# Flamingo gated cross-attention block: x loaded a second time in transposed form, the queries projected from it with centred weights, and the order of the steps rewritten

## The chip, the cores and the metric

One core of a Trainium2 chip. The metric is the device time of one execution in microseconds (us). The kernel before takes 1874.98 us, the median of 3 runs (1874.72 to 1876.57).

## The reference, cut to what matters

`x` is 64 x 128 x 256, the context `c` as well, all float32. There are 16 heads of 16 columns.

```python
x = x + tanh(g_xattn) * xattn(layernorm(x), c, c)     # causal, softmax, Wo, bo
x = x + tanh(g_ffn) * ffn(layernorm(x))
# layernorm(x) = (x - mean) / sqrt(var + 1e-5), over the 256 columns
# xattn: scores = (q Wq)(k Wk)^T / sqrt(16), masked above the diagonal
# ffn: h = silu(x w1 s1) * (x w2 s2); h = gelu(h h1 s); h = gelu(h h2 s); h w3 s
#      256 -> 1024 -> 1024 -> 1024 -> 256
```

## The kernel before, in words

**Blocks and stages.** The 64 batches go in 32 blocks of two (ROWS = 2, 256 tokens). A block passes two stages, attention and FFN. One pass of the loop, `body(n)`, runs attention of block n, FFN of block n-1 and the head of the attention of block n+1 (its loads, its projections, its first scores), interleaved. The passes -1 and 0 have no FFN and bring in the weights; the last two leave parts out.

**The order.** The string ORDER holds 203 steps, written out by hand as one list. Every engine walks the same list in its own loop and picks the steps it has a part in, so one list sets the order on each engine and on SP's DMA queue. Nothing else schedules: engines meet only through semaphores. `L2.3` is step L2 with index 3; a `+` means the next block. On TensorE: L1 (index 0 to 7, eight matmuls each), L2 and L3 (0 to 7, sixteen each), L4 (0 to 3, eight each) are the FFN layers, line 925; each hidden value is held in two parts, hi and lo, and multiplied twice, so a block has 352 FFN matmuls. Q, K, V project (line 860), X transposes normalised x (line 870), S.u writes the scores of eight heads to two banks (line 899), PV.t multiplies probabilities with v (line 916), To and X2 transpose (line 1011), O projects the output (line 860). The f32 matmuls of line 860 appear in the trace as two instructions each, so Q is 8 instructions and O.0 is 4.

**What surrounds them.** On ACT: a1 is tanh of L1's result (line 794), h writes ha_hi (785), a2 and a3 are Gelu to `full` and to hi (769, 771), e.t is four exps (749), x, q, k, v, to, x2 evacuate PSUM. ACT loads a function table when it goes from Gelu to Exp and back; Tanh and Exp share one, copies need none. On DVE: g and f are the two products of the gated layer (597, 604), w2 and w3 write the lo part of a pair (611), s.t masks and scales scores (570), m.t is the maximum and the exp's bias (577, 579), nh.u sums heads (588, 590), st takes mean and variance of x (530 to 536), nx normalises x (541), o.k adds the residual and takes the statistics of x1 (669 to 677), n2 normalises x1 (683), x2 writes x2T_lo (688), y scales the FFN output. On POOL: l.k writes ha_lo (476), p.t splits probabilities in two f16 parts (442, 444), nm divides heads, st and n2 are the powers -1/2 (484, 487), v writes the third part of v (465), rx adds the bias to the residual, z adds the residual of the FFN. On SP: lx, lr, lc load x, the residual and c; kw, qw write the parts of k and q to DRAM and kr, qr read them back spread over the partitions (`place_parts`); D.t transposes p_parts to pT; mv copies x1; sy stores y; W.k loads weights.

**Banks.** The steps To, O, X2, X, Q, K and V (MISC_STEPS) take turns on two PSUM banks in the order of the list; `before_step` (line 242) makes each wait until the step two places before it has been evacuated. The FFN has three banks, `before_ffn` (269) waits in the same way; PV has one bank, the scores two.

**The chain for the queries.** SP loads x_in; DVE takes the statistics (`head_stats`), POOL the power, DVE normalises x_in in place (`head_norm`), TensorE transposes it (X+), ACT copies it to xT (x+), TensorE projects it (Q+) in one step of both column halves, ACT and DVE write q's hi and lo part, SP writes and places them for S.0.

**Waits of TensorE that matter.** L2.0 waits for l.0 to l.7 one tile after another (`tile_split`); L3.0 waits for w2.0 to w2.3, one before each pair of tiles (four matmuls to a pair), so the last comes before its thirteenth matmul; L4.k waits for w3.k; L1.0 waits for x2.1 on DVE; a1.k with k over 3 waits for l.(k-4); a3.6 waits for w3.1.

In the passes -1 and 0, ACT rounds eleven weight chunks (`round_chunk`, 727) and DVE tests their low bits (635, 638), at the steps W.k; the first FFN step waits for all of them.

Of the kernel before, what the change touches and what calls it, by code (L numbers as in the profile page):

```python
# [47 lines left out]
def program(nc, x, cT_in, g_xattn, g_ffn, attn_w, bo, w_all, s1, s2, h1s, h2s, w3s, out):  # L48
# [27 lines left out]
    with ExitStack() as ctx:  # L76
# [432 lines left out]
        def _(dve):  # L509
            dve.wait_ge(pool_const, 7)  # L510
# [33 lines left out]
            def split_head(n, kind):  # L544

                parts, hi_ready, lo_ready = (q_parts, q_hi_ready, q_lo_ready) if kind == "q" else \
                    (k_parts, k_hi_ready, k_lo_ready)
                wait(dve, hi_ready, n + 1)
                dve.tensor_tensor(parts[:, 1],
                                  work[step_bank(kind.upper())][:].rearrange("p (m r t) -> p r m t", m=KE, r=ROWS),  # L550
                                  parts[:, 0].bitcast(F32), ALU.subtract).then_inc(lo_ready, 1)
# [158 lines left out]
        def _(act):  # L710
# [18 lines left out]
            def head_step(n, kind):  # L729
                use = step_bank(kind.upper())  # L730
                src = work[use][:].rearrange("p (m t) -> p m t", m=KE)
                if kind == "x":

                    wait(act, xT_ready, n + 1)
                    wait(act, q_ready, n)
                    act.activation(xT[:], src, ACT.Copy).then_inc(xT_copied, 1)
                if kind in ("q", "k"):

                    wait(act, q_ready if kind == "q" else k_ready, n + 1)
                    wait(act, q_written if kind == "q" else k_written, 16 * n)  # L740
                    act.activation((q_parts if kind == "q" else k_parts)[:, 0],
                                   work[use][:].rearrange("p (m r t) -> p r m t", m=KE, r=ROWS), ACT.Copy)\
                        .then_inc(q_hi_ready if kind == "q" else k_hi_ready, 1)
# [112 lines left out]
        def _(pe):  # L856
# [6 lines left out]
            def head_step(n, kind, k):  # L863
                bank_ = work[step_bank(kind, k)]
                before_step(pe, n, kind, k)
                if kind == "X":
                    wait(pe, xn_ready, ROWS * n + ROWS)
                    for kt in range(KE):
                        for b in range(ROWS):
                            last = pe.transpose(bank_[:, (kt * ROWS + b) * P:(kt * ROWS + b + 1) * P],  # L870
                                                x_in[:, b, kt * P:(kt + 1) * P], ident[:])
                    last.then_inc(xT_ready, 1)
                if kind in ("Q", "K"):
# [2 lines left out]
                    w, src = (wq, xT) if kind == "Q" else (wk, cT)
# [206 lines left out]
```

## Time and profile before

| | |
|---|---|
| median of 3 runs | 1874.98 us |
| profiled execution, its own time | 1874.17 us |
| its span, first to last instruction | 1872.4 us |
| mean granted TensorE clock | 0.981 |
| busy: PE, PEld, ACT, DVE, POOL | 95, 91, 65, 64, 48% |
| DMA engines, mean busy share of the steady slices | 0.4 |
| chain that ended last | PE 67%, POOL 12%, issue 9%, DVE 7% |

How to read it: times are in us unless marked ns; PE is TensorE's matmuls, PEld its weight loads, L925 is line 925 of the kernel. Matmuls overlap: a row of 0.28 us starts 0.12 us after the one before it, so distances between starts tell more than durations. The execution shown was profiled; 1.8 us of its time lie outside the span.

### The profile page before, as it was taken

The numbers are of one execution on the slowest core, as the hardware profiler recorded it, in microseconds if no ns is written. First come the engines' busy times: TensorE is split into PE (matmuls) and PEld (weight loads), VectorE is DVE, ScalarE is ACT, GpSimd is POOL, SyncE is SP. The second block draws the span as 40 slices with busy tenths as digits, with TensorE's granted clock in tenths as the row PEclk, the third lists the DMA queues.
The fourth block names the chain that finished last, engine by engine and source line by source line (L and its number), as shares of the span: only waits on it lengthen the run. The fifth ranks groups of instructions, "written<-read, shape, count | busy, mean of one in ns | idle before, by whom it ended". The sixth has DMA issues, their size and how long they took to land.

```text
span 1872.4 us, 47622 instructions
## 1 busy us (share of the span) xinstructions
PE 1781.1 (95%) x15746; PEld 1708.9 (91%) x15746; DVE 1198.4 (64%) x2706; ACT 1221.9 (65%) x2952; POOL 901.5 (48%) x1131
## 2 busy tenths in 40 slices
PE   2489999999999999999999999999999999999998
PEld 2389999999999999999999999999999999999998
DVE  3857666567666567666667766667766667766652
ACT  2566666677666677666667666667666667666664
POOL 2544544455544455544455554455454455454441
PEclk7689999999999999999999999999999999999999
DMA  6834444444445443445443444444444444444430
GB/s 227 250 86 119 124 118 131 105 119 105 124 117 134 109 117 99 129 113 139 112 120 98 123 117 131 119 116 105 119 118 123 126 110 108 116 123 118 126 55 18
DMA packets 395102, 223.04 MB, mean 119 GB/s; under 512 B 286784, under 2 KB 377152, under 8 KB 393536
## 3 DMA queue, kind: packets, MB, share of 16 engines
q1 hardware_dynamic: 390336, 222.38, 45.1%
q10 hardware_dynamic: 4736, 0.28, 0.2%
q8 instruction: 17, 0.28, 0.1%
q14 instruction: 13, 0.11, 0.0%
HBM read 105.14 MB, written 41.94 MB: 79 GB/s over the span
## 4 chain that ended last, share of the span: by engine, by line
PE 67%; POOL 12%; issue 9%; DVE 7%; ACT 3%; ACTq 1%; DMA 1%; POOLq 1%; SPq 0%; DVEq 0%
PE ffn L925 49%; PE work L860 11%; POOL ha_lo L476 8%; POOL y L493 2%; DVE negmax L577 2%; DVE probs L570 2%; PE s_bank L899 2%; PE pv L916 2%; ACT probs L749 2%; PE work L1011 1%; POOL p_parts L442 1%; DVE ha_lo L611 1%; ACTq L720 1%; PE work L870 1%; DMA pT<-p_parts 0%
## 5 line engine op out<-in xcount | busy, mean ns | idle before, releaser
L925 PE MATMUL ffn<-ha_hi,W 128*128 128x256 f32 x2048 | 500.8, 286 | 19.3 <-POOL ha_lo L476 19.3
L925 PE MATMUL ffn<-hb_hi,W 128*128 128x256 f32 x2048 | 513.7, 291 | 1.2 <-DVE hb_lo L611 1.2
L925 PE MATMUL ffn<-ha_lo,W 128*128 128x256 f32 x2048 | 488.7, 279 | 0.0
L925 PE MATMUL ffn<-hb_lo,W 128*128 128x256 f32 x2048 | 488.1, 279 | 0.0
L925 PEld LDWEIGHTS ffn<-ha_hi,W 128*128 128x128 f32 x2048 | 384.1, 188 | 28.3 <-POOL ha_lo L476 26.0
L749 ACT ACTIVATE probs<-probs,exp_bias 128x128 f32<-128x128 f32 x1024 | 320.9, 390 | 113.4 <-DVE exp_bias L579 111.9
L925 PEld LDWEIGHTS ffn<-hb_hi,W 128*128 128x128 f32 x2048 | 384.5, 188 | 4.0 <-DVE hb_lo L611 1.6
L925 PEld LDWEIGHTS ffn<-hb_lo,W 128*128 128x128 f32 x2048 | 384.8, 188 | 2.4
L925 PEld LDWEIGHTS ffn<-ha_lo,W 128*128 128x128 f32 x2048 | 384.6, 188 | 0.0
L444 POOL TENSOR_TENSOR p_parts<-probs,p_parts 128x512 f16<-128x512 f32 x256 | 313.2, 1224 | 20.5
L442 POOL CAST p_parts<-probs 128x512 f16<-128x512 f32 x256 | 159.2, 622 | 327.7 <-ACT probs L749 311.3
L769 ACT ACTIVATE full<-ffn,h2s_col 128x256 f32<-128x256 f32 x256 | 121.7, 475 | 224.2 <-PE ffn L925 223.8
L925 PE MATMUL ffn<-x2T_hi,W 128*128 128x256 f32 x1024 | 252.1, 287 | 6.2 <-issue 4.2
L925 PE MATMUL ffn<-x2T_lo,W 128*128 128x256 f32 x1024 | 245.1, 280 | 0.0
L454 POOL TENSOR_TENSOR heads<-head_sum,rden 128x128 f32<-128x128 f32 x128 | 57.2, 447 | 338.6 <-DVE head_sum L590 338.6
L925 PEld LDWEIGHTS ffn<-x2T_hi,W 128*128 128x128 f32 x1024 | 193.6, 189 | 12.6 <-DVE x2T_lo L688 5.8
L476 POOL TENSOR_TENSOR ha_lo<-full,ha_hi 128x256 fp32r<-128x256 f32 x256 | 184.2, 736 | 36.6 <-ACT ha_hi L785 33.4
L611 DVE TENSOR_TENSOR hb_lo<-full,hb_hi 128x512 fp32r<-128x512 f32 x128 | 93.9, 733 | 165.6 <-ACT hb_hi L771 165.6
L925 PEld LDWEIGHTS ffn<-x2T_lo,W 128*128 128x128 f32 x1024 | 193.8, 189 | 0.0
L611 DVE TENSOR_TENSOR ha_lo<-full,ha_hi 128x512 fp32r<-128x512 f32 x128 | 88.1, 688 | 139.4 <-ACT ha_hi L771 139.4
L577 DVE TENSOR_REDUCE negmax<-probs 128x4 f32<-128x512 f32 x256 | 173.3, 677 | 2.2
L570 DVE SCALAR_TENSOR_TENSOR probs<-s_bank,causal 128x512 f32<-128x512 f32 x256 | 166.6, 681 | 9.4 <-PE s_bank L899 7.4
(86 smaller groups left out, 3169.1 us busy)
## 6 DMA issues: line engine op xcount, KB each, us to landing
k<-k_saved SPq DMA_DIRECT2D x256, 128.0 KB, 2.9
q<-q_saved SPq DMA_DIRECT2D x256, 128.0 KB, 2.7
k_saved<-k_parts SPq DMA_DIRECT2D x32, 512.0 KB, 3.1
q_saved<-q_parts SPq DMA_DIRECT2D x32, 512.0 KB, 2.6
wnat<-in_ffn_w SPq DMA_DIRECT2D x11, 1024.0 KB, 7.0
x_in<-in_x SPq DMA_DIRECT2D x32, 256.0 KB, 2.9
cT<-in_ctx_T SPq DMA_DIRECT2D x32, 256.0 KB, 2.7
xres<-in_x SPq DMA_DIRECT2D x32, 256.0 KB, 2.7
```

Source lines behind the costliest of these rows:

```text
L442: pool.tensor_copy(p_parts[:, t % 2, 0], probs[:, t % PSLOTS]).then_inc(p_hi_ready, 1)
L444: pool.tensor_tensor(p_parts[:, t % 2, 1], probs[:, t % PSLOTS], p_parts[:, t % 2, 0], ALU.subtract)\
L454: pool.tensor_tensor(heads[:, b, at:at + PAIR * D].rearrange("p (h d) -> p h d", h=PAIR), head_sum[:, u % 2], rden[:, b, (u % 2) * PAIR:(u ...
L476: pool.tensor_tensor(ha_lo[:, k], full[:, k % 4], ha_hi[:, k], ALU.subtract)\
L493: pool.tensor_tensor(y[:, k], y[:, k], x1_prev[:, k], ALU.add).then_inc(y_ready, 1)
L570: dve.scalar_tensor_tensor(probs[:, slot], s_bank[t % SBANKS][:].rearrange("p (h t) -> p h t", h=4), SCALE, causal[:].unsqueeze(1).broadca ...
L577: dve.tensor_reduce(negmax[:, slot], probs[:, slot], AX_X, ALU.max, negate=True).then_inc(max_ready, 1)
L611: dve.tensor_tensor(lo[:, 2 * p:2 * p + 2], f, hi[:, 2 * p:2 * p + 2], ALU.subtract)\
L749: last = act.activation(probs[:, slot, h], probs[:, slot, h], ACT.Exp, bias=exp_bias[:, slot, h:h + 1])
L769: act.activation(full[:, 2 * (p % 2) + r], src, ACT.Gelu, scale=scales[:, m:m + 1])\
L860: last = pe.matmul(dst, lhsT(kt), rhs(kt), start=kt == 0, stop=kt == KE - 1)
L925: return pe.matmul(dst, w, h, **flags)
```

## The change

- The host lays out x a second time, transposed (`x_T`, per block 128 x 2 x 256). SP loads it to xT (`load_xT`, step lt+). X+, x+ and nx+ are gone: no normalisation of x ahead of the projection, no transposes, no copy.
- The mean goes into the weights: at the start TensorE takes the mean of wq over its input rows (a matrix of 1/256 times wq) and DVE subtracts it (`centre_queries`). 1/std goes into the mask: `mask` scales by rstd instead of the constant SCALE, which is folded into var_eps; st+ on POOL also waits for the masks of the block before.
- Q+ becomes Q.0+ and Q.1+, each one column half of 128 in its own bank, and so do q.0+ and q.1+ on ACT and DVE.
- The whole list ORDER is new. Both orders, as they stand, and the core of the diff:

```diff
-    W.0 l.0 W.1 s.2 s.3 kr.1 lx+ D.0 D.1 e.0 e.1 g.0 f.0 L1.0 L1.1 a1.0 a1.1 l.1 L1.2 g.1 h.0 a1.2 f.1 g.2 L1.3 L1.4
-    L1.5 f.2 h.1 g.3 L1.6 a1.3 S.2 h.2 f.3 L1.7 a1.4 h.3 l.2 l.3 PV.0 PV.1 g.4 a1.5 L2.0 f.4 l.4 h.4 L2.1 g.5 l.5
-    a1.6 h.5 f.5 g.6 a1.7 h.6 W.2 f.6 h.7 g.7 f.7 L2.2 L2.3 L2.4 l.6 l.7 m.2 L2.5 m.3 W.3 W.4 p.2 s.4 s.5 p.3 nh.0
-    D.2 m.4 st+ X+ m.5 e.2 e.3 nx+ PV.2 D.3 w2.0 PV.3 W.5 e.4 e.5 nh.1 a2.0 w2.1 S.3 a2.1 a2.2 L2.6 s.6 mv To.0 x+
-    L2.7 a2.3 a2.4 nm.0 lc+ p.4 s.7 O.0 m.6 nm.1 D.4 D.5 to.0 w2.2 K+ m.7 a2.5 L3.0 L3.1 PV.4 PV.5 L3.2 a2.6 p.5 p.6
-    p.7 Q+ sy V+ w2.3 a2.7 L3.3 L3.4 PV.6 PV.7 W.6 L3.5 e.6 To.1 D.6 o.0 L3.6 X2.0 e.7 kw+ k+ a3.0 w3.0 D.7 a3.1
-    nh.2 O.1 W.7 q+ qw+ a3.2 a3.3 W.8 L3.7 nh.3 nm.2 n2.0 kr.0+ nm.3 qr.0+ v+ lr+ W.9 a3.4 qr.1+ S.0+ L4.0 w3.1 w3.2
-    o.1 to.1 W.10 a3.5 X2.1 x2.0 L4.1 L4.2 L4.3 n2.1 rx+ S.1+ p.0+ s.0+ z.0 z.1 a3.6 m.0+ a3.7 w3.3 s.1+ m.1+ x2.1
-    y.0 y.1 p.1+
+    kr.1 W.0 e.0 L1.0 L1.1 e.1 lt+ L1.2 L1.3 a1.0 W.1 L1.4 L1.5 D.0 D.1 L1.6 p.1 s.2 s.3 L1.7 PV.0 PV.1 S.2 l.0 l.1
+    g.0 L2.0 lc+ f.0 W.2 g.1 a1.1 h.0 f.1 W.3 D.2 D.3 a1.2 g.2 f.2 g.3 l.2 h.1 a1.3 l.3 L2.1 L2.2 lx+ L2.3 f.3 h.2
+    g.4 a1.4 L2.4 f.4 h.3 g.5 a1.5 L2.5 h.4 f.5 g.6 S.3 a1.6 f.6 h.5 g.7 f.7 l.4 m.2 a1.7 h.6 h.7 e.2 m.3 e.3 PV.2
+    PV.3 l.5 nh.0 L2.6 L2.7 l.6 l.7 s.4 s.5 a2.0 a2.1 a2.2 K+ p.2 w2.0 p.3 m.4 mv nm.0 L3.0 a2.3 W.4 W.5 e.4 D.4 m.5
+    e.5 nh.1 D.5 s.6 L3.1 To.0 PV.4 w2.1 PV.5 L3.2 s.7 O.0 Q.0+ m.6 m.7 Q.1+ w2.2 w2.3 a2.4 L3.3 W.6 p.4 p.5 W.7 V+
+    PV.6 nm.1 a2.5 a2.6 a2.7 k+ e.6 PV.7 L3.4 p.6 p.7 nm.2 e.7 to.0 To.1 W.8 kw+ L3.5 o.0 q.0+ O.1 L3.6 L3.7 D.6
+    q.1+ a3.0 D.7 nh.2 W.9 st+ W.10 nh.3 w3.0 S.0+ nm.3 qw+ kr.0+ X2.0 X2.1 v+ n2.0 o.1 sy a3.1 n2.1 w3.1 to.1 w3.2
+    qr.0+ a3.2 a3.3 L4.0 L4.1 s.0+ lr+ L4.2 a3.4 qr.1+ rx+ m.0+ p.0+ w3.3 a3.5 a3.6 a3.7 x2.0 L4.3 s.1+ m.1+ x2.1
+    S.1+ y.0 y.1 z.0 z.1
```

```diff
             def load_x(n):
 
-                hold(xT_ready, n)
+                hold(stats_ready, ROWS * n)
                 sp.dma_start(x_in[:], x[bass.ds(n * ROWS, ROWS)].rearrange("b p e -> p b e")).then_inc(x_loaded, 16)
+
+            def load_xT(n):
+
+                hold(q_ready, KE * n)
+                sp.dma_start(xT[:], xT_in[bass.ds(n, 1)].rearrange("a p k t -> p (a k) t")).then_inc(xT_loaded, 16)
...
-            load_x(0)
+            load_xT(0)
             sp.dma_start(aw[:].rearrange("p w k e -> p (w k e)"), attn_w[:, :]).then_inc(attn_w_in, 16)
             load_c(0)
+            load_x(0)
...
                     if kind == "st" and here:
                         wait(pool, var_ready, blk + 1)
+                        wait(pool, masked_ready, NQ * blk)
                         pool.tensor_tensor(rstd[:], var_eps[:], minus_half[:], ALU.pow).then_inc(rstd_ready, 1)
...
-                dve.tensor_scalar(var_eps[:], moments[:, :, 1], EPS, None, ALU.add).then_inc(var_ready, 1)
-
-            def head_norm(n):
-                wait(dve, rstd_ready, n + 1)
-                for b in range(ROWS):
-                    dve.tensor_scalar(x_in[:, b], x_in[:, b], moments[:, b, 0:1], rstd[:, b:b + 1],
-                                      ALU.subtract, ALU.mult).then_inc(xn_ready, 1)
...
+                dve.tensor_scalar(var_eps[:], moments[:, :, 1], EPS, 1.0 / SCALE ** 2, ALU.add, ALU.mult)\
+                    .then_inc(var_ready, 1)
+
+            def centre_queries():
+
+                dve.wait_ge(attn_w_in, 16)
+                dve.wait_ge(wq_mean, 1)
+                dve.tensor_tensor(wq, wq, ffn[1][:, 0:E].unsqueeze(1).broadcast_to([P, KE, E]), ALU.subtract)\
+                    .then_inc(wq_centred, 1)
+
+            def split_query(n, m):
+
+                wait(dve, q_hi_ready, KE * n + m + 1)
+                dve.tensor_tensor(q_parts[:, 1, :, m],
+                                  work[step_bank("Q", m)][:, 0:TOK].rearrange("p (r t) -> p r t", r=ROWS),
+                                  q_parts[:, 0, :, m].bitcast(F32), ALU.subtract).then_inc(q_lo_ready, 1)
...
-                dve.scalar_tensor_tensor(probs[:, slot], s_bank[t % SBANKS][:].rearrange("p (h t) -> p h t", h=4), SCALE,
+                if t == 0:
+                    wait(dve, rstd_ready, n + 1)
+                dve.scalar_tensor_tensor(probs[:, slot], s_bank[t % SBANKS][:].rearrange("p (h t) -> p h t", h=4),
+                                         rstd[:, t // QROW:t // QROW + 1],
                                          causal[:].unsqueeze(1).broadcast_to([P, 4, P]), ALU.mult, ALU.add)\
...
-                if kind == "X":
-                    wait(pe, xn_ready, ROWS * n + ROWS)
-                    for kt in range(KE):
-                        for b in range(ROWS):
-                            last = pe.transpose(bank_[:, (kt * ROWS + b) * P:(kt * ROWS + b + 1) * P],
-                                                x_in[:, b, kt * P:(kt + 1) * P], ident[:])
-                    last.then_inc(xT_ready, 1)
...
+                if kind == "Q":
+                    if isinstance(n, int) and n == 0:
+                        pe.wait_ge(wq_centred, 1)
+                    wait(pe, xT_loaded, (n + 1) * 16)
+                    project(bank_[:, 0:TOK], lambda kt: wq[:, kt, k * P:(k + 1) * P], lambda kt: xT[:, kt])\
+                        .then_inc(q_ready, 1)
...
                 if first == 0:
+                    pe.wait_ge(attn_w_in, 16)
+                    project(ffn[1][:, 0:E], lambda kt: mean_of[:], lambda kt: wq[:, kt]).then_inc(wq_mean, 1)
                     body(-1, ffn_on=False, attn=False)
```

The evacuation of the queries on ACT (`queries`) is split by column half as on DVE.

## Rows read from the trace of the kernel before

**Rows 1.** The page, busy time: engine, us (share of the span), instructions.

```profile
PE 1781.1 (95%) x15746; PEld 1708.9 (91%) x15746; DVE 1198.4 (64%) x2706; ACT 1221.9 (65%) x2952; POOL 901.5 (48%) x1131
```

**Rows 2.** Busy time by stretches: stretch, length, engines, clock, DMA share, GB/s.

```profile
165.30:1783.90 1618.60, 1599.09 (x14275) 1539.44 (x14271) 1060.86 (x2437) 1093.45 (x2669) 803.78 (x1016) 1.00 0.45 117
```

**Rows 3.** Timeline of PE: start us, us, engine, line, operation.

```profile
1014.31 0.60 PE L870 MATMUL work<-ident,x_in 128*128 128x128 f32 x4
1014.75 0.57 PE L916 MATMUL pv<-vs,pT 128*128 128x49 bf16 x16
...
1740.44 0.60 PE L870 MATMUL work<-ident,x_in 128*128 128x128 f32 x4
```

**Rows 4.** Timeline of PE from the end of L1.7 into L2.0.

```profile
1057.20 0.58 PE L916 MATMUL pv<-vs,pT 128*128 128x49 bf16 x16
1057.62 0.37 PE L925 MATMUL ffn<-ha_hi,W 128*128 128x256 f32 x1
1057.83 0.28 PE L925 MATMUL ffn<-ha_lo,W 128*128 128x256 f32 x1
...
1059.28 0.28 PE L925 MATMUL ffn<-ha_lo,W 128*128 128x256 f32 x1
1060.15 0.39 PE L925 MATMUL ffn<-ha_hi,W 128*128 128x256 f32 x1 [0.59 <-POOL ha_lo L476]
```

**Rows 5.** Timeline of POOL, the last ha_lo of the same block.

```profile
1059.37 0.72 POOL L476 TENSOR_TENSOR ha_lo<-full,ha_hi 128x256 fp32r<-128x256 f32 x1 [0.37 <-ACT ha_hi L785]
```

**Rows 6.** Timeline of PE, S.1 and the first matmul of L1.

```profile
1048.05 0.66 PE L899 MATMUL s_bank<-k,q 64*128 64x128 f32 x8
1048.78 0.39 PE L925 MATMUL ffn<-x2T_hi,W 128*128 128x256 f32 x1
```

**Rows 7.** Timeline of PE: O.0 behind L2.7, a projection of 8, L3.0.

```profile
1019.94 1.02 PE L860 MATMUL work<-aw,oT 128*128 128x256 f32 x4
1020.80 1.89 PE L860 MATMUL work<-cT,aw 128*128 128x256 f32 x8
1022.34 0.47 PE L925 MATMUL ffn<-hb_hi,W 128*128 128x256 f32 x1
```

**Rows 8.** Timeline of ACT and DVE: a2.7, the table load, exps, w2.3.

```profile
1020.92 0.48 ACT L769 ACTIVATE full<-ffn,h1s_col 128x256 f32<-128x256 f32 x1
1021.28 0.48 ACT L771 ACTIVATE hb_hi<-ffn,h1s_col 128x256 fp32r<-128x256 f32 x1
1021.78 1.28 ACT L749 ACT_TABLE_LOAD   x1
1023.08 2.46 ACT L749 ACTIVATE probs<-probs,exp_bias 128x128 f32<-128x128 f32 x8
...
1021.79 0.69 DVE L611 TENSOR_TENSOR hb_lo<-full,hb_hi 128x512 fp32r<-128x512 f32 x1 [0.72 <-ACT hb_hi L771]
```

**Rows 9.** Timeline of ACT at the start.

```profile
18.14 1.28 ACT L722 ACT_TABLE_LOAD   x1 [18.14 <-issue]
```

**Rows 10.** Groups by line: busy us, mean ns | idle before, releaser.

```profile
L604 DVE SCALAR_TENSOR_TENSOR full<-ffn,half_s,full 128x256 f32<-128x256 f32 x256 | 123.9, 484 | 9.0
L597 DVE SCALAR_TENSOR_TENSOR full<-full,ffn 128x256 f32<-128x256 f32 x256 | 107.4, 419 | 37.8 <-ACT full L794 34.6
L465 POOL TENSOR_TENSOR vs<-v_rest,vs 128x512 bf16<-128x512 f32 x32 | 50.7, 1584 | 48.5 <-DVE vs L563 48.5
L487 POOL TENSOR_TENSOR rstd<-var_eps,minus_half 128x1 f32<-128x1 f32 x64 | 36.6, 572 | 98.3 <-DVE var_eps L677 98.3
```

**Rows 11.** Waits: who waited for whom, us in total, times, longest.

```profile
ACT probs L749 <- DVE exp_bias L579: 111.9, 119, 6.2
PE ffn L925 <- POOL ha_lo L476: 19.3, 33, 0.6
```

**Rows 12.** Timeline of SP and PE: the placing of q's first row, S.0.

```profile
1035.58 2.46 SPq L327 DMA_DIRECT2D q<-q_saved  x4
1043.35 0.66 PE L899 MATMUL s_bank<-k,q 64*128 64x128 f32 x8
```

More of the change, by code:

```diff
@@ L102, in program @@
         ones = sb("ones", [P, 1])
+        mean_of = sb("mean_of", [P, P])
         minus_half = sb("minus_half", [P, ROWS])
@@ L363, in body @@
                         load_x(blk)
+                    if kind == "lt" and here and not (isinstance(blk, int) and blk < 2):
+                        load_xT(blk)
                     if kind == "lr" and here:
@@ L387, in _ @@
             load_x(1)
+            load_xT(1)
             load_c(1)
@@ L418, in _ @@
             pool.memset(minus_half[:], -0.5).then_inc(pool_const, 1)
-            pool.wait_ge(pool_const, 4)
+            pool.memset(mean_of[:], 1.0 / E).then_inc(pool_const, 1)
+            pool.wait_ge(pool_const, 5)
             pool.affine_select(out=ident[:], in_=ident[:], compare_op=ALU.not_equal, fill=1.0, base=0,
@@ L509, in _ @@
         def _(dve):
-            dve.wait_ge(pool_const, 7)
+            dve.wait_ge(pool_const, 8)
             def scale_constants():
@@ L535, in head_stats, with split_keys @@
                 wait(dve, moments_ready, ROWS * n + ROWS)
-                dve.tensor_scalar(var_eps[:], moments[:, :, 1], EPS, None, ALU.add).then_inc(var_ready, 1)
-            def head_norm(n):
-                wait(dve, rstd_ready, n + 1)
-                for b in range(ROWS):
-                    dve.tensor_scalar(x_in[:, b], x_in[:, b], moments[:, b, 0:1], rstd[:, b:b + 1],
-                                      ALU.subtract, ALU.mult).then_inc(xn_ready, 1)
[L544 to L551, printed above, removed]
+                dve.tensor_scalar(var_eps[:], moments[:, :, 1], EPS, 1.0 / SCALE ** 2, ALU.add, ALU.mult)\
[10 more added lines that the diff above has]
+                                  q_parts[:, 0, :, m].bitcast(F32), ALU.subtract).then_inc(q_lo_ready, 1)
+            def split_keys(n):
+                wait(dve, k_hi_ready, n + 1)
+                dve.tensor_tensor(k_parts[:, 1],
+                                  work[step_bank("K")][:].rearrange("p (m r t) -> p r m t", m=KE, r=ROWS),
+                                  k_parts[:, 0].bitcast(F32), ALU.subtract).then_inc(k_lo_ready, 1)
             def values(n):
@@ L646, in body @@
                         head_stats(blk)
-                    if kind == "nx" and here:
-                        head_norm(blk)
-                    if kind == "nx" and isinstance(n, int) and n == -1:
+                    if kind == "st" and isinstance(n, int) and n == -1:
                         scale_constants()
@@ L691, in body @@
                             .then_inc(x2lo_ready, 1)
-                    if kind in ("q", "k") and here:
-                        split_head(blk, kind)
+                    if kind == "q" and here:
+                        split_query(blk, k)
+                    if kind == "k" and here:
+                        split_keys(blk)
                     if kind == "v" and here:
                         values(blk)
+            centre_queries()
             body(-1, ffn_on=False, attn=False)
@@ L727, in round_chunk, with queries, keys @@
                 act.activation(W[:, i * CHUNK:(i + 1) * CHUNK], wnat[:, i % STAGES], ACT.Copy).then_inc(chunk_rounded, 1)
[L729 to L743, printed above, removed]
+            def queries(n, m):
+                wait(act, q_ready, KE * n + m + 1)
+                wait(act, q_written, 16 * n)
+                act.activation(q_parts[:, 0, :, m],
+                               work[step_bank("Q", m)][:, 0:TOK].rearrange("p (r t) -> p r t", r=ROWS), ACT.Copy)\
+                    .then_inc(q_hi_ready, 1)
+            def keys(n):
+                wait(act, k_ready, n + 1)
+                wait(act, k_written, 16 * n)
+                act.activation(k_parts[:, 0],
+                               work[step_bank("K")][:].rearrange("p (m r t) -> p r m t", m=KE, r=ROWS), ACT.Copy)\
+                    .then_inc(k_hi_ready, 1)
             def exps(n, t):
@@ L836, in body @@
                             .then_inc(x2hi_ready, 1)
-                    if kind in ("x", "q", "k") and here:
-                        head_step(blk, kind)
+                    if kind == "q" and here:
+                        queries(blk, k)
+                    if kind == "k" and here:
+                        keys(blk)
                     if kind == "v" and here:
@@ L865, in head_step @@
                 before_step(pe, n, kind, k)
[L866 to L873 removed]
+                if kind == "Q":
[4 more added lines that the diff above has]
+                        .then_inc(q_ready, 1)
+                if kind == "K":
                     if isinstance(n, int) and n == 0:
                         pe.wait_ge(attn_w_in, 16)
[L876 to L877 removed]
+                    wait(pe, cT_loaded, (n + 1) * 16)
                     for m in range(KE):
[L879 to L881 removed]
+                        last = project(bank_[:, m * TOK:(m + 1) * TOK], lambda kt: wk[:, kt, m * P:(m + 1) * P],
+                                       lambda kt: cT[:, kt])
+                    last.then_inc(k_ready, 1)
                 if kind == "V":
@@ L1029, in run @@
                 body(BLOCKS, attn=False, next_head=False)
-            pe.wait_ge(pool_const, 7)
+            pe.wait_ge(pool_const, 8)
             run(False, 0)
@@ L1061 @@
         "x": x,
+        "x_T": x.reshape(b // ROWS, ROWS * s, e // P, P).transpose(0, 3, 2, 1),
         "ctx_T": ctx.reshape(b // ROWS, ROWS * s, e // P, P).transpose(0, 3, 2, 1),
```

20 lines of the change are left out of this document (8 added, 12 removed).

## The prediction

> **What bounds the kernel now.** I read the page first. TensorE is busy 95% of the span and the next engine 65% [rows 1], so the question is whether it is really full. The busy time by stretches says so for the steady part: between 165.3 and 1783.9 us it is busy 99% at a granted clock of 1.00, while DVE, ACT and POOL are at 66, 68 and 50% [rows 2]. A busy PE hides short waits, though, so I went to the order of instructions in one block and read starts, not durations. The transposes of x start at 1014.31 us in one block and at 1740.44 us 13 blocks later [rows 3]: (1740.44 - 1014.31) / 13 = 55.86 us a block. The FFN matmuls start 0.12 us apart (12 of them from 1057.83 to 1059.28) [rows 4], so 352 are some 42 us; the reader should see that this stream, the attention matmuls between its pieces and a few gaps are the whole block.
>
> Two gaps matter. In L2.0 one matmul starts at 1059.28 and the next at 1060.15, 0.75 us late; the waits put it down to POOL's ha_lo (19.3 us in 33 times) [rows 11], and the matmul behind it starts 0.1 us late too, as behind every interruption (0.21 instead of 0.12 after PV) [rows 4]: 0.86 us a block. POOL's last ha_lo began at 1059.37 and had itself waited for ACT's ha_hi [rows 5], the end of the chain L1.7, a1.7, g.7, f.7, h.7, l.7. And from S.1 to the next L1 pass 0.73 us, more than the 0.66 of its eight matmuls [rows 6], though elsewhere a group starts some 0.07 before the last one ends: 0.14 us.
>
> **The change part by part.** All against the profiled execution, 1874.17 us, 0.04% below the median of 1874.98.
>
> Removed, transposes of x: 1014.31 to 1014.75, 0.44 us of PE a block [rows 3], on the path in full. With it go the copy of xT on ACT and two normalisations on DVE; both engines have a third of their time free, so I count nothing for them.
>
> The query projection in two steps: eight half-matmuls become four and four at the same 0.216 us (O.0: 0.86 us for four), no more PE work. ACT and DVE each evacuate twice 256 columns instead of once 512, about 0.1 us of fixed cost each, covered by their idle time. But the first step of a pair frees the other's bank late: Q.1 takes O.0's bank and waits for o.0 on DVE, and starts 2 x 0.86 us after O.0 [rows 7]. o.0 needs O.0's four matmuls, 0.9 us or so with its drain, and 0.48 us of its own: nearly equal. I take 0.1 us; ends 0 and 0.5.
>
> The mask now scales by a column (rstd) and not by a constant. Nearest rows: 484 ns with a column against 419 ns with a constant, both on 256 columns [rows 10]. So 0 to 0.07 us more for each of 8 masks a block, on DVE with its slack: nothing, as long as it does not sit in the chain named below.
>
> Moved, S.2: it stood between L1.6 and L1.7 and now follows L1.7 and PV.1. The chain from L1.7's last matmul (1057.20) to POOL's last ha_lo (1059.37 + 0.72 = 1060.09) is 2.89 us; TensorE needs 0.42 for PV and 1.8 for the first seven tiles of L2.0, hence the gap [rows 4, 5]. With another 0.6 to 0.7 us of S.2 in it the gap shrinks to 0.05 to 0.15. In exchange L1.7 and PV.0 come 0.7 us earlier against f.4 and the transposed probabilities, which may be late: bounds 0 and 0.7, and I take 0.2 for what is left of both. Moved, x2.0 and X2.0: together with X2.1 ahead of L4.0. DVE then has x2.0 behind it before s.1, and X2.1 no longer lies inside L4, so L4 and S.1 run with DVE ahead of them: the 0.14 us go.
>
> Interruptions of the FFN stream per block fall from 13 to 10 (counted in the two orders), each return costs 0.09 us [rows 4], but PV in front of S gives 0.08 back: -0.2.
>
> Moved, st: POOL's rstd goes from between p.3 and p.4 to between nm.2 and nm.3, and now also waits for the masks; nm.3 waits behind it, and To.1 for nm.3. DVE runs st between nh.2 and nh.3, when V is still on TensorE, so the 0.7 us are covered; without that cover they would be on the path.
>
> The queue of SP: the load of x^T takes the place of the load of x ahead of D.0, the load of x goes behind D.3, c ahead of D.2, and the store of y between kr.0 and qr.0. Each is one issue of about 0.4 us. The placing of q is issued until 1035.58 + 2.46 = 1038.04 and S.0 starts at 1043.35 [rows 12]: 5.3 us are left for the last piece to land, and a store more in front takes 0.4 of them. Covered. 0.25 MB more a block is nothing on DMA engines busy 45% [rows 2].
>
> Two more table switches on ACT: e.4 and e.5 now stand between a2.3 and a2.4, so Gelu, Exp, Gelu. A switch costs 1.30 us: gelu ends 1021.76, load 1021.78 to 1023.06, exp starts 1023.08 [rows 8]. Between the ends of L2.3 and L2.7 TensorE has four steps of 1.89 and S.3 and PV, 8.6 us; ACT has a2.2 and a2.3 (four activations 0.36 apart), a switch, eight exps (2.46), a switch, a2.4 and a2.5: 1.4 + 1.3 + 2.5 + 1.3 + 1.4 = 7.9. It arrives 0.7 us early [rows 8]. K alone now stands between L2.7 and L3.0, so w2.3 (done 1022.48, 2.54 after L2.7's end) is wanted after K and twelve matmuls of L3.0: 8 x 0.216 + 12 x 0.118 = 3.15 us, 0.6 us to spare [rows 7, 8]. Cost nothing; if the cover of 0.7 + 0.6 us is gone, every further us is on the path. The Trainium skill (ScalarE: Activation LUTs, What ACT_TABLE_LOAD costs) puts 1380 ns of drain on top of 1283 ns of load for every switch; the load agrees with the row, the drain does not show in it. By that page two more switches last 2.76 us longer than the rows have them, and the sum would be about 1881 us.
>
> The start: Q waited for xT until 20.27 us, since ACT's first load comes at 18.14 [rows 9]; now K and Q.0 are done by then and only Q.1 is left, 1.4 us gained. Against it, the weight tests W.3 and W.10 move ahead of m.2 and of nh.3, and To.1, O.1, o.1, n2.1 then run one after another behind W.10. I take +3 us; ends -1.4 and +6.
>
> Sum a block: -0.44 (X) - 0.86 (ha_lo) - 0.14 (S.1) - 0.2 (interruptions) + 0.3 (0.2 left of the moved S.2, 0.1 for Q.1) = -1.34. Over 31 blocks with the transposes in 30: -41.5 + 0.4, with the start +3: -38. **1874 - 38 = 1836 us.**
>
> **The rivals.**
> (a) The end of the block becomes the chain. w3.0, V's evacuation (1.1), POOL's third part of v (1.6), rstd2 (0.6), n2.0 (0.4), o.1 with its statistics (1.2), rstd2 (0.6), n2.1 (0.4) and w3.1 (0.7) are now one file on DVE and POOL (POOL's pieces from [rows 10]; DVE's are estimates, 0.4 to 0.5 us for 256 columns and 0.7 for 512, after [rows 8, 10]), and a3.6 waits for w3.1, then e.0, p.0, p.1 and all of l. With w3.0 starting 1.6 us behind PV.7 that is 8.9 us; TensorE reaches the end of L3.7 after four steps, To.1 and O.1, about 8.9 us too. A slip of 0.5 us comes back whole in L2.0: 1836 + 31 x 0.5 = 1852. For it: no slack, and it is DVE and POOL work in a row. Against: none of these engines is full.
> (b) The ha_lo gap stays, because p.1 ahead of l.0 sets it and not L1.7. Then 0.66 of the 0.86 us stay: 1836 + 20 = 1856. Against: POOL waited for ACT before its last ha_lo [rows 5].
> (c) Slower: L3.0 waits for ACT. If each switch also drained for as long as it loads (2 x 1.3) and e.4 waited for its bias as the exps do now (111.9 us in 119 waits, 0.94 each [rows 11]), w2.3 slips 3.5 us against a cover of 1.3: 2.2 us a block, 1836 + 69 = 1905. The point of no gain is a slip of 1.3 + 38 / 31 = 2.5 us. Against: the switch row shows no drain. The skill's page named above gives the drain.
> (d) Nothing new waits and the start gains: -1.64 x 31 - 1 = 1822.
>
> **How the numbers follow.** Forecast 0.52, (a) 0.20, (b) 0.12, (c) 0.06, (d) 0.10. The range 1820 to 1858 holds the forecast with its bounds (Q.1, the remainder, the start), (a), (b) and (d). A measurement of this kernel can tell about 0.2% (4 us) from no change. Faster 0.92; within 0.2%: 0.03, from (c) with half its slip; slower 0.05.
>
> **What would show it.** Block period 54.4 to 54.6 us; no matmul of x on ident; L925 waiting for POOL ha_lo under 5 us in all, not 19.3; six table loads a block on ACT where there were four; L1 of the first block starting near 101 us. Wrong if PE waits in L3.0 for hb_lo, in Q.1 for DVE's x, or if a3.6 starts later than 0.2 us behind L3.7.

## The result, and the profile after

The changed kernel takes 1853.45 us, the median of 4 runs (1852.85 to 1859.93), beside 1875.78 us (1874.72 to 1876.92) for the kernel before: a ratio of 0.9889 with the interval 0.9874 to 0.9904. The profiled execution took 1853.97 us. The run of 1859.93 us had a mean granted TensorE clock of 0.931, the other three 0.978 to 0.980. The direction is as forecast and the time lies in the range, but 22 us were gained where 38 were expected.

The page after, busy time, and below it the line of the chain that ended last:

```profile
PE 1775.5 (96%) x15622; PEld 1691.6 (91%) x15622; DVE 1159.0 (63%) x2675; ACT 1291.6 (70%) x3014; POOL 894.7 (48%) x1132
...
PE 74%; DVE 9%; issue 7%; POOL 5%; ACT 3%; ACTq 1%; DMA 1%; POOLq 0%; SPq 0%; DVEq 0%
```

PE lost 124 instructions (32 x 4 transposes go, four for the mean of wq come) and 5.6 us of busy time [rows 1]; the span lost 20. POOL's share of the chain fell from 12 to 5%, and DVE's rose from 7 to 9%: one wait went, and something on DVE came. The steady part by stretches looks full, as before [rows 2]:

```profile
165.00:1783.90 1618.90, 1615.28 (x14367) 1543.78 (x14367) 1037.29 (x2438) 1179.47 (x2774) 806.89 (x1031) 1.00 0.47 123
```

The period is read from starts again. O.0 on PE's timeline, 13 blocks apart: (1732.25 - 1017.09) / 13 = 55.01 us. Counted from block 3 to block 29 it is 55.01 as well, and 55.81 in the kernel before.

```profile
1017.09 1.02 PE L885 MATMUL work<-aw,oT 128*128 128x256 f32 x4
...
1732.25 1.02 PE L885 MATMUL work<-aw,oT 128*128 128x256 f32 x4
```

So a block gained 0.80 us, not 1.34. The whole adds up so: from the first matmul of L2 in the first block to that in the last, 1721.7 us before and 1698.5 after, -23.1; that stretch starts 2.9 us later (112.6, not 109.7); the tail is equal; -20.2 for the span.

Where TensorE waits now, from the waits after (who waited for whom, us, times, longest):

```profile
PEld work L885 <- DVE x L689: 11.3, 29, 0.4
PEld ffn L948 <- DVE full L626: 9.0, 30, 0.3
PEld ffn L948 <- POOL ha_lo L487: 5.1, 23, 0.6
PE ffn L948 <- POOL ha_lo L487: 0.9, 2, 0.4
ACT full L817 <- POOL ha_lo L487: 10.6, 30, 0.4
```

The 19.3 us of ha_lo [rows 11] are down to 0.9 on PE; on the weight loads (PEld) they are down from 26.0 to 5.1. Three small waits a block are there now, two of them new, and the weight loads show them, not the matmuls. The starts on PE's timeline size each. First L1.7, in one block:

```profile
1044.78 0.28 PE L948 MATMUL ffn<-x2T_hi,W 128*128 128x256 f32 x1
1044.89 0.28 PE L948 MATMUL ffn<-x2T_lo,W 128*128 128x256 f32 x1
1045.26 0.39 PE L948 MATMUL ffn<-x2T_hi,W 128*128 128x256 f32 x1
1045.49 0.28 PE L948 MATMUL ffn<-x2T_lo,W 128*128 128x256 f32 x1
```

From 1044.89 to 1045.26 are 0.37 us instead of 0.12, and the next start is 0.23 behind instead of 0.12: 0.25 of waiting and 0.11 of refill, 0.36 us. L1.7 takes the bank that f.4 frees on DVE. Then what is left of the ha_lo gap, in L2.0:

```profile
1049.01 0.28 PE L948 MATMUL ffn<-ha_lo,W 128*128 128x256 f32 x1
1049.29 0.38 PE L948 MATMUL ffn<-ha_hi,W 128*128 128x256 f32 x1
1049.51 0.28 PE L948 MATMUL ffn<-ha_lo,W 128*128 128x256 f32 x1
```

0.28 and 0.22 instead of 0.12 twice, 0.26 us in this block. The mean of blocks 3 to 28 is 0.24, and counted in the same way it was 0.90 before (the one block of [rows 4] has 0.86). Third, O.0, Q.0 and Q.1 (the last two are the x8), with the residual on DVE that frees Q.1's bank:

```profile
1017.09 1.02 PE L885 MATMUL work<-aw,oT 128*128 128x256 f32 x4
1017.95 2.15 PE L885 MATMUL work<-xT,aw 128*128 128x256 f32 x8
1019.75 0.47 PE L948 MATMUL ffn<-hb_hi,W 128*128 128x256 f32 x1
```

```profile
1018.43 0.48 DVE L689 SCALAR_TENSOR_TENSOR x<-work,gates,xres 128x256 f32<-128x256 f32 x1 [6.10 <-PE work L885]
```

The eight last 1.80 us (1019.75 - 1017.95), where a projection of eight without a wait, K's, lasted 1.54 [rows 7]: 0.15 of waiting in front of Q.1's first matmul and 0.10 behind it, 0.25 us. Together 0.36 + 0.24 + 0.25 = 0.85 us, where the sum had 0.3.

Why is L1.7's bank late? POOL's, ACT's and DVE's timelines give the chain:

```profile
1039.71 1.44 POOL L505 TENSOR_TENSOR y<-y,x_prev 128x256 f32<-128x256 f32 x2
1041.10 0.61 POOL L453 CAST p_parts<-probs 128x512 f16<-128x512 f32 x1
1041.79 1.17 POOL L455 TENSOR_TENSOR p_parts<-probs,p_parts 128x512 f16<-128x512 f32 x1
1042.92 2.84 POOL L487 TENSOR_TENSOR ha_lo<-full,ha_hi 128x256 fp32r<-128x256 f32 x4
```

```profile
1043.76 0.48 ACT L817 ACTIVATE full<-ffn,half_s 128x256 f32<-128x256 f32 x1 [0.35 <-POOL ha_lo L487]
```

```profile
1044.27 0.42 DVE L619 SCALAR_TENSOR_TENSOR full<-full,ffn 128x256 f32<-128x256 f32 x1 [0.43 <-ACT full L817]
1044.72 0.48 DVE L626 SCALAR_TENSOR_TENSOR full<-ffn,half_s,full 128x256 f32<-128x256 f32 x1
```

z.0 and z.1 (the FFN's residual, 1.44 us) stand on POOL ahead of p.1 and of l.0; a1.4 needs l.0's buffer; g.4 and f.4 follow, and f.4 ends at 1045.20, just before L1.7's delayed matmul. Nobody needs z early. That is a reading so far; two runs below take it to the test.

### The profile page after: what moved, and what is told of

It is laid out like the page before. It is cut to its first block, busy times and chain, and to the rows that moved or that the text cites. A ratio compares the mean times of both kernels' runs of the same rounds, so it can differ in the third digit from the quotient of the medians.

```text
span 1852.2 us, 47792 instructions
## 1 busy us (share of the span) xinstructions
PE 1775.5 (96%) x15622; PEld 1691.6 (91%) x15622; DVE 1159.0 (63%) x2675; ACT 1291.6 (70%) x3014; POOL 894.7 (48%) x1132
## 4 chain that ended last, share of the span: by engine, by line
PE 74%; DVE 9%; issue 7%; POOL 5%; ACT 3%; ACTq 1%; DMA 1%; POOLq 0%; SPq 0%; DVEq 0%
PE ffn L948 54%; PE work L885 12%; PE s_bank L922 3%; PE pv L939 3%; DVE probs L591 2%; DVE negmax L599 2%; POOL y L505 2%; ACT probs L772 2%; POOL ha_lo L487 1%; POOL p_parts L453 1%; DVE full L626 1%; ACTq L743 1%; DVE full L619 1%; PE work L1034 1%; ACT full L817 1%
## 5 line engine op out<-in xcount | busy, mean ns | idle before, releaser
L948 PE MATMUL ffn<-ha_hi,W 128*128 128x256 f32 x2048 | 495.4, 284 | 0.9 <-POOL ha_lo L487 0.9
L453 POOL CAST p_parts<-probs 128x512 f16<-128x512 f32 x256 | 173.8, 679 | 488.5 <-ACT probs L772 482.1
L455 POOL TENSOR_TENSOR p_parts<-probs,p_parts 128x512 f16<-128x512 f32 x256 | 305.8, 1194 | 20.4
L591 DVE SCALAR_TENSOR_TENSOR probs<-s_bank,rstd,causal 128x512 f32<-128x512 f32 x256 | 184.5, 742 | 25.1 <-PE s_bank L922 25.1
L792 ACT ACTIVATE full<-ffn,h1s_col 128x256 f32<-128x256 f32 x256 | 121.9, 476 | 54.4 <-PE ffn L948 53.6
L817 ACT ACTIVATE full<-ffn,half_s 128x256 f32<-128x256 f32 x256 | 120.7, 472 | 48.6 <-PE ffn L948 37.8
```

What stands on the lines that cost most here:

```text
L453: pool.tensor_copy(p_parts[:, t % 2, 0], probs[:, t % PSLOTS]).then_inc(p_hi_ready, 1)
L455: pool.tensor_tensor(p_parts[:, t % 2, 1], probs[:, t % PSLOTS], p_parts[:, t % 2, 0], ALU.subtract)\
L792: act.activation(full[:, 2 * (p % 2) + r], src, ACT.Gelu, scale=scales[:, m:m + 1])\
L817: act.activation(full[:, k % 4], ffn[use][:, 0:TOK], ACT.Tanh, scale=half_s1[:, k:k + 1])\
L948: return pe.matmul(dst, w, h, **flags)
```

## The experiments

All ratios are against the kernel before on the same chip, and a period is the mean from O.0 of block 3 to O.0 of block 29 in the profiled execution. The kernel before has 55.81 us, the changed one 55.01. The period is the cleaner measure: the first matmul of L2 starts anywhere from 110.6 to 114.9 us in these versions, and that moves the time as well.

**Which half of the change earned what.** The first try kept the old list, with the new steps in the places of the old ones.

```diff
- ... D.2 m.4 st+ X+ m.5 e.2 e.3 nx+ PV.2 ... To.0 x+ L2.7 ... p.7 Q+ sy ... W.7 q+ qw+ ...
+ ... D.2 m.4 st+ m.5 e.2 e.3 PV.2 ... To.0 L2.7 ... p.7 Q.0+ Q.1+ sy ... W.7 q.0+ q.1+ qw+ ...
```

> The change without its new order: the old list with X, x and nx taken out, the load of x transposed beside that of x, and Q, q in two steps where they stood as one. Theory 1 (transposes lie on TensorE's path in full, and everything else of the gain comes from the order): the block period falls by 0.44 us from 55.8 to 55.4, the ha_lo gap of 0.75 us in L2.0 stays, time about 1874 - 13.6 + 0 to 3 = 1861 to 1864. Rival 2 (the order gives nothing, the functional change all of it): 1853.

Measured: 2081.14 us (2079.49 to 2082.96), ratio 1.109 (1.1072 to 1.1109), period 62.5 us. The expectation missed by far. POOL's timeline shows the cause, and its waits the sum:

```profile
1007.01 0.71 POOL L497 TENSOR_TENSOR rstd<-var_eps,minus_half 128x2 f32<-128x2 f32 x1 [8.60 <-DVE probs L592]
1007.69 0.40 POOL L466 TENSOR_TENSOR heads<-head_sum,rden 128x128 f32<-128x128 f32 x1
```

```profile
POOL rstd L497 <- DVE probs L592: 266.7, 31, 8.7
```

rstd of the next block now waits for the last mask of this one, since the masks read it. In its old place it stands in front of nm.0 and p.4 and holds POOL for 8.6 us in each of 31 blocks. Not all of the 6.7 us a block need be this wait: this version also differs from the one before in Q's steps and in the turns on the banks, and TensorE's granted clock was 0.96 to 0.97 from 300 us on, with 1.00 in the kernel before. But st+ has to move with the functional change. The second try moved st+ behind nh.2 and kept the rest of the old list, with Q in one step, and X+ as an empty step that only keeps the turns on the banks.

```diff
- D.2 m.4 st+ X+ m.5 e.2 e.3 nx+ PV.2 ... To.0 x+ L2.7 ... D.7 a3.1 nh.2 O.1
+ D.2 m.4 X+ m.5 e.2 e.3 nx+ PV.2 ... To.0 x+ L2.7 ... D.7 a3.1 nh.2 st+ O.1
-                            "X2": (x2lo_ready, ROWS, k + 1), "X": (xT_copied, 1, 1), "Q": (q_lo_ready, 1, 1),
+                            "X2": (x2lo_ready, ROWS, k + 1), "Q": (q_lo_ready, 1, 1),
```

> The functional change alone, in the old list: x loaded transposed, centred weights, 1/std in the mask, no transposes, but Q in one step and each bank as before; only st moves, from in front of m.4 to behind nh.2, since POOL may not overwrite rstd before the last mask. Theory 1: 0.44 us a block less than before and the ha_lo gap of 0.75 us still there: 55.4 us a block, 1861 to 1864 us. Rival (the gap was the transposes' doing, or all of the gain is the functional change): 1853 or less. Second rival (st's two microseconds on DVE in the new place delay q and k): 1870 or more.

Measured: 1865.27 us (1863.92 to 1867.26), ratio 0.9955 (0.9941 to 0.9969), period 55.47: 0.34 us a block less than before, and 1.3 us above the expected range. The ha_lo gap is all there, and the mask takes longer (waits; groups):

```profile
PE ffn L933 <- POOL ha_lo L489: 19.5, 33, 0.6
```

```profile
L588 DVE SCALAR_TENSOR_TENSOR probs<-s_bank,rstd,causal 128x512 f32<-128x512 f32 x256 | 182.6, 745 | 11.1 <-PE s_bank L907 6.9
```

0.44 us of transposes go. The distance from the last matmul of S.1 to L1, where L1 waits for x2.1 behind the masks on DVE, grows from 0.34 to 0.40 us in the mean, by the 0.06 that a mask of 745 ns takes more than one of 681. The rest of the gain, 55.47 - 55.01 = 0.46 us, is the new order's (with Q in two steps).

**S.2 back ahead of L1.7.**

```diff
- L1.6 p.1 s.2 s.3 L1.7 PV.0 PV.1 S.2 l.0
+ L1.6 p.1 s.2 s.3 S.2 L1.7 PV.0 PV.1 l.0
```

> The changed kernel with S.2 put back between L1.6 and L1.7. Theory 1 (S.2 behind L1.7 closes the ha_lo gap and opens the wait of L1.7 for f.4): L1.7's wait of 0.25 us and its refill go (-0.36), the gap in L2.0 comes back to 0.6 to 0.8 (+0.6), one interruption more (+0.1): +0.3 to +0.4 us a block, 1863 to 1866. Rival: S.2's place does not matter, the gap was closed by x2.0's and e.0's new places: 1853 or less.

Measured: 1866.34 us (1865.47 to 1866.88), ratio 0.9947 (0.993 to 0.9963), period 55.40. The wait at L1.7 is gone and the gap in L2.0 is back, as in the waits before [rows 11]:

```profile
PE ffn L949 <- POOL ha_lo L488: 19.1, 33, 0.6
```

The move of S.2 alone is worth 0.39 us a block: the gap's 0.90 us, less what is left of it (0.24) and less the new wait at L1.7 (0.37), make 0.29, and the one interruption more the other 0.1.

**z.0 and z.1 out of the chain.** They go behind l.7 of the next pass, so POOL no longer has 1.44 us of them ahead of p.1 and l.0; the last block's are done at the end.

```diff
- ... PV.3 l.5 nh.0 L2.6 L2.7 l.6 l.7 s.4 s.5 ... x2.1 S.1+ y.0 y.1 z.0 z.1
+ ... PV.3 l.5 nh.0 L2.6 L2.7 l.6 l.7 z.0 z.1 s.4 s.5 ... x2.1 S.1+ y.0 y.1
-                        wait(pool, y_scaled, ROWS * j + k + 1)
-                        wait(pool, x1_moved, 16 * (j + 1))
+                        wait(pool, y_scaled, ROWS * (j - 1) + k + 1)
+                        wait(pool, x1_moved, 16 * j)
```

> The changed kernel with POOL's z.0 and z.1 (1.44 us, the sum of y and x1) moved from in front of p.1 and l.0 to behind l.7, that is into the next pass. Theory 1 (L1.7 waits for f.4, f.4 for a1.4, a1.4 for l.0 on POOL, and POOL is late because of z): both waits go, 0.36 and 0.21 us a block: 54.4 us, time about 1853 - 18 = 1836. Rival (the chain is DVE's g and f, or ACT, and not POOL): the wait of L1.7 stays, 1850 to 1853.

Measured: 1842.05 us (1841.52 to 1843.08), ratio 0.9817 (0.98 to 0.9833), period 54.65. L1.7 waits no more, and that is all: L2.0's wait stays in full (0.26 us in the mean, 0.24 in the changed kernel), which is why the gain is less than expected. PE's timeline there, and POOL's last ha_lo of the block, in this version and in the changed kernel:

```profile
1042.15 0.28 PE L953 MATMUL ffn<-ha_lo,W 128*128 128x256 f32 x1
1042.42 0.39 PE L953 MATMUL ffn<-ha_hi,W 128*128 128x256 f32 x1
```

```profile
1041.63 0.73 POOL L488 TENSOR_TENSOR ha_lo<-full,ha_hi 128x256 fp32r<-128x256 f32 x1 [0.20 <-ACT ha_hi L813]
```

```profile
1048.49 0.74 POOL L487 TENSOR_TENSOR ha_lo<-full,ha_hi 128x256 fp32r<-128x256 f32 x1 [0.22 <-ACT ha_hi L808]
```

In both it waits for ACT and not for POOL's queue, and from the start of L1.7's last matmul to its end pass 3.03 us in both (3.01 in the kernel before). So L2.0 waits for the chain that starts with L1.7 itself, as in the kernel before [rows 5], and z stood only ahead of L1.7. My expectation that both waits hang on z was half wrong. No run shortened that chain by itself.

**Q.1 later.** Sixteen matmuls of L3.3 between Q.0 and Q.1 give DVE's o.0 time.

```diff
- O.0 Q.0+ m.6 m.7 Q.1+ w2.2 w2.3 a2.4 L3.3 W.6
+ O.0 Q.0+ m.6 m.7 w2.2 w2.3 a2.4 L3.3 Q.1+ W.6
```

> The changed kernel with Q.1 moved behind L3.3, so that o.0 has two more microseconds to free the bank. Theory 1: the wait of 0.15 us and its refill of 0.1 us in Q.1 go, 0.25 us a block: 1845 to 1846. Rival (the bank of O.0 is not what holds Q.1, or q's later placing holds S.0): 1853 or slower, with PE waiting for DMA q in S.0.

Measured: 1845.88 us (1844.18 to 1846.86), ratio 0.9834 (0.9818 to 0.9851), period 54.75. The row "PEld work <- DVE x" is gone from the waits, and the block is 0.26 us shorter; the starts gave 0.25.

**Both together.**

> The changed kernel with z.0, z.1 behind l.7 and Q.1 behind L3.3, both of the single moves together. Theory 1 (the waits are separate): 1853.5 - 11.4 - 7.6 = 1834.5, 54.4 us a block. Rival (they share a chain, so that one move uncovers the other's wait): 1838 to 1842.

Measured: 1832.57 us (1831.84 to 1833.39), ratio 0.9779 (0.9763 to 0.9795), period 54.32, 0.69 us a block less than the changed kernel. This is the fastest version of the case. The chain that ended last, from its page:

```profile
PE 91%; issue 2%; DVE 2%; DMA 1%; ACTq 1%; POOL 1%; SPq 1%; ACT 1%; POOLq 0%; DVEq 0%
```

```profile
PEld ffn L953 <- POOL ha_lo L488: 3.4, 14, 0.6
```

67% of PE before, 74% after, 91% here. The two moves add up (0.36 + 0.26 = 0.62 of 0.69).

**Does a wait absorb work?** Four transposes of a weight tile that nobody needs, of the same size as the removed ones (0.44 us), go into the bank of the step behind them: once ahead of Q.0, in the cover of o.0, and once ahead of K.

```diff
+                if kind == "Q" and k == 0 and not (isinstance(n, int) and n == 0):
+                    for kt in range(KE):
+                        for b in range(ROWS):
+                            pe.transpose(bank_[:, (kt * ROWS + b) * P:(kt * ROWS + b + 1) * P],
+                                         wk[:, b, kt * P:(kt + 1) * P], ident[:])
```

> The changed kernel with four transposes of a weight tile put back on TensorE between O.0 and Q.0, into Q.0's bank, which Q.0 overwrites (0.44 us a block of work that nobody needs). Theory 1 (o.0 gets that time too, so Q.1's wait of 0.25 us with its refill goes): +0.19 us a block, 1858 to 1860. Rival (work on TensorE costs its length anywhere): +0.44, 1866 to 1868.

> The changed kernel with the same four transposes of a weight tile put back in front of K instead, into K's bank, which K overwrites. Nothing on another engine waits to be caught up there; the cover of w2.3 only grows. Theory 1 (the transposes were on TensorE's path in full): +0.44 us a block, 1866 to 1868. Rival (removed work of TensorE is partly waiting anyway, wherever it stands): 1858 or less, as for the transposes behind O.0.

Measured: ahead of Q.0 1855.92 us (1854.58 to 1857.61), ratio 0.9906 (0.9889 to 0.9922), period 55.10; ahead of K 1864.05 us (1862.59 to 1865.33), ratio 0.9941 (0.9924 to 0.9958), period 55.42. The same work costs 0.41 us in one place and 0.09 in the other. Where it stands in front of Q.1's wait, that wait of 0.25 us is no longer in the trace, so most of the work is hidden by it; theory 1 had +0.19, and the other 0.1 is not explained. Both times lie some 2 us below their expected ranges, and in both the first L2 starts earlier than in the changed kernel (111.3 and 110.8 us, not 112.6). The run with K also prices the removed transposes from the other side: 0.41 for my 0.44.

**Four table loads instead of six.** e.4 and e.5 ahead of a2.0, so that ACT goes from Exp to Gelu and back once less.

```diff
- s.4 s.5 a2.0 a2.1 a2.2 K+ p.2 w2.0 p.3 m.4 mv nm.0 L3.0 a2.3 W.4 W.5 e.4 D.4 m.5 e.5 nh.1
+ s.4 s.5 e.4 e.5 a2.0 a2.1 a2.2 K+ p.2 p.3 m.4 mv nm.0 L3.0 a2.3 W.4 W.5 D.4 m.5 w2.0 nh.1
```

> The changed kernel with e.4 and e.5 put ahead of a2.0 on ACT and w2.0 behind m.5 on DVE: four table loads a block instead of six, 2.6 us less of ACT. Theory 1 (the two extra loads are covered): no gain, 1852 to 1856. Rival 3 (they cost what the forecast missed, 0.5 us a block): 1838 to 1845. By the Trainium skill's total for a switch, 2.66 us, ACT would win 5.3 us a block, and the rival's case would be the stronger.

Measured: 1855.63 us (1854.41 to 1858.73), ratio 0.9906 (0.9889 to 0.9922), period 55.01. The block is as long as with six; the 2 us more come from the start (first matmul of L2 at 114.9, not 112.6). The groups show the loads, of the changed kernel and then of this one:

```profile
L792 ACT ACT_TABLE_LOAD x93 | 119.3, 1283 | 2.1
L772 ACT ACT_TABLE_LOAD x92 | 118.0, 1283 | 1.6
```

```profile
L793 ACT ACT_TABLE_LOAD x62 | 79.5, 1283 | 1.1
L773 ACT ACT_TABLE_LOAD x61 | 78.3, 1283 | 1.1
```

**The start.** My reason for it was W.3, W.9 and W.10 standing ahead of attention's own steps. This run moves them behind e.3, v and o.1 in the version with both edits.

```diff
- f.1 W.3 D.2 ... m.3 e.3 PV.2 ... nh.2 W.9 st+ W.10 nh.3 ... X2.1 v+ n2.0 o.1 sy
+ f.1 D.2 ... m.3 e.3 W.3 PV.2 ... nh.2 st+ nh.3 ... X2.1 v+ W.9 n2.0 o.1 W.10 sy
```

> Both moves (z behind l.7, Q.1 behind L3.3), and in the list the weight steps W.3 behind e.3, W.9 behind v and W.10 behind o.1, as they lay in the old list; that touches pass 0 alone. Theory 1 (the start lost 3 us because the weight tests stand in front of m.2 and nh.3, and To.1, O.1, o.1 and n2.1 follow W.10 one after another): 1832.6 - 3 = 1829 to 1831, the first L2 at 109 us instead of 112. Rival (the tests only change places with other waits on DVE): 1832 to 1834.

Measured: 1835.09 us (1832.42 to 1836.06), ratio 0.9783 (0.9767 to 0.9799), period 54.39. The expectation missed: the first L1 starts at 101.62 us, with the tests in their places at 100.79. In the chain ahead of it a weight chunk's load (7.69 us) and the transposes of pT (4.95 us) have in part taken the tests' place. The first matmul of L1 on PE's timeline, before and after:

```profile
98.76 0.58 PE L925 MATMUL ffn<-x2T_hi,W 128*128 128x256 f32 x1 [4.20 <-issue]
```

```profile
101.82 0.58 PE L948 MATMUL ffn<-x2T_hi,W 128*128 128x256 f32 x1 [4.71 <-issue]
```

That start also differs between versions that leave the start alone: it is 101.82 in the changed kernel, and 100.25 to 101.35 in the six other versions with the new list that touch neither the weight tests nor the table loads. So the loss at the start is 1.5 to 3 us. The new list cannot be its only cause: the functional change in the old list, with the tests in their old places, starts L1 at 100.46 us, already 1.7 later than before, and L2 at 110.6 (109.7 before). The cause is open.

## Why the prediction was right or wrong

**Transposes, -0.44: right.** No PE row works on x with ident, and the same amount of work put back ahead of K costs 0.41.

**The ha_lo gap, -0.86: about three quarters.** 0.66 of 0.90 us went and 0.24 stays, 0.13 of waiting and 0.11 of refill. The text said itself that the gap "shrinks to 0.05 to 0.15", which the wait does, and the sum then took it as gone, with its refill, and had only 0.2 for what is left of it and L1.7's wait together. (The chain of 2.89 us was read from 1057.20, where PV.0 starts; L1.7's last matmul starts at 1057.08, so it is 3.01. What was to be left came from the gap, and does not hang on it.)

**S.1 to L1, -0.14, and interruptions, -0.2: as forecast** in the starts after, -0.14 and some -0.24; neither was tried by itself. The starts of blocks 3 to 28 also show three terms that the sum does not have. L4.3 had waited for w3.3 (DVE ha_lo) in some blocks, 0.17 us in the mean with the refill, and waits no more. Against that, the undisturbed FFN matmuls stand a little further apart (in L3.0 and L3.1, for instance, 0.118 us after and 0.115 before), +0.15 us a block, and X2.0, now behind S.0, takes 0.06 more. Why the distance differs is open. The three nearly cancel, which is luck.

**The +0.3 is the step that failed.** "I take 0.2 for what is left of both" and "I take 0.1 us" for Q.1: measured are 0.36 at L1.7, 0.24 left in L2.0 and 0.25 at Q.1, 0.85 in place of 0.3. Those 0.55 us are the shortfall of a block (1.34 - 0.80 = 0.54), and over 31 blocks 17 us, the miss (1853.45 against 1836). The values lay inside my bounds of 0.7 and 0.5, and were taken from their low end. For L1.7 I had the bound of 0.7, but not the chain: I did not follow what stands on POOL ahead of l.0, where z.0, z.1 and p.1 wait in a row. Moving z away gave 0.36 back, so this cause is shown. For Q.1 I set 0.9 + 0.48 of o.0 against 2 x 0.86 and called them nearly equal; that was the right chain, but o.0 starts 1.34 us behind O.0 (1018.43 - 1017.09), not 0.9, and with its 0.48 ends 0.1 behind the 1.72. Putting Q.1 later gave 0.26. And I priced a short wait at its own length, though my own rows had the refill of 0.1 us behind each wait [rows 4]: 0.3 of the 0.85 is refill.

**The mask by column, "nothing as long as it does not sit in the chain": right with its condition.** It takes 742 ns, 61 more than before, inside the bound of 0.07. In the new order it is not in the chain; in the old one it is, and cost 0.06.

```profile
L591 DVE SCALAR_TENSOR_TENSOR probs<-s_bank,rstd,causal 128x512 f32<-128x512 f32 x256 | 184.5, 742 | 25.1 <-PE s_bank L922 25.1
```

**st+ moved, 0: right, and by more than I saw.** I named its wait for the masks and what queues behind it in the new place, but not that the old place was closed to it: there POOL stood 8.6 us a block in it, and I take it for most of the 7 us a block between the two runs with the old list (62.53 and 55.47), which differ in two more things.

**Two more table switches, 0: shown** by the run with four loads. ACT's timeline after has exp, load, Gelu without a pause:

```profile
1005.48 0.39 ACT L772 ACTIVATE probs<-probs,exp_bias 128x128 f32<-128x128 f32 x1
1005.88 1.28 ACT L792 ACT_TABLE_LOAD   x1
1007.18 0.47 ACT L792 ACTIVATE full<-ffn,h1s_col 128x256 f32<-128x256 f32 x1
```

A switch is 1.31 us from the end of the exp to the start of Gelu (1007.18 - 1005.87), load included. The drain of 1380 ns that the Trainium skill (ScalarE: Activation LUTs, What ACT_TABLE_LOAD costs) adds to it is not in these rows either. In one pass alone, that of the last block's attention, which has no next head and so no K between L2.7 and L3.0, the cover is gone and L3 does wait for hb_lo: PE's timeline of that pass, twice 0.55 us.

```profile
1780.64 0.39 PE L948 MATMUL ffn<-hb_hi,W 128*128 128x256 f32 x1 [0.39 <-DVE hb_lo L633]
...
1781.77 0.39 PE L948 MATMUL ffn<-hb_hi,W 128*128 128x256 f32 x1 [0.38 <-DVE hb_lo L633]
```

The interval before the last L2 grew by 1.05 us (47.5 to 48.6), while the others shrank; the two waits are 1.1 us of what changed there. So the slower rival's mechanism exists, in one pass of 32; I had put the cover to K in words and not followed the pass that lacks K.

**The start, +3: right in size (2.9 to the first L2) by luck, its reason not borne out.** Moving the weight tests gained nothing, and with the old list 0.9 of the 2.9 us is there already.

**The rivals.** (a) did not come: a3.6 starts at 1032.92, 0.16 us behind 1032.76, where S.0 follows L3.7. (b) did not come; POOL's queue with p.1 in it was the right place to look, but it struck at L1.7. (c) only in that one pass. (d), with no new wait, is 1822; the version without the two waits took 1832.57, since some of the ha_lo wait and the later start remain. Of what I had named as a sign of error, one came true: PE waits in Q.1 for DVE's x. Of the signs of being right, the block period of 54.4 to 54.6 us did not come (55.01); the transposes, the six table loads and the ha_lo waits on PE did.

## What to carry to other kernels

Before an engine's step is moved earlier, list everything that stands ahead of its releaser on the releaser's own queue, and write down when each could be done at the latest; here 1.44 us of work that nobody needed stood in such a place, and moving it gave 0.36 of the 0.54 us a block that were missing. Price every new wait at its length plus the refill, and take an unknown from the bound its own chain gives, not from the low end. A stall that goes uncovers the next one: after a long gap is closed, look at the starts between matmuls and at the waits of the weight loads, since the busy share says 99 to 100% either way.

## What the runs showed that was not expected

- A wait costs TensorE more than its length. In a stream of FFN matmuls that start 0.118 us apart, the second matmul behind a wait starts 0.22 to 0.23 us behind the first (1045.26 to 1045.49, 1049.29 to 1049.51); in the projections, 0.216 apart, it is 0.32.
- Short waits show at PEld and not at PE: the row of L1.7's wait is 9.0 us at PEld and has none at PE, while 30 blocks of 0.36 us are 10.8.
- A mask with a column of rstd as its scale takes 742 ns for 512 columns, with a constant 681.
- Ahead of a wait of 0.25 us (refill included), 0.44 us of independent matmuls cost 0.09 us a block.
